# Causal attention in a decoder kernel: the next score before half an output tile instead of behind it

## The reference, cut to what matters

```
kqv = (x @ Wqkv + bqkv).reshape(b, s, 3, 16, 32)
q, k, v = kqv[:, :, 0], kqv[:, :, 1], kqv[:, :, 2]
scores = einsum('bsnh,btnh->bnst', k, q) / sqrt(32)
scores = triu(scores) + -10000.0 * tril(ones, k=-1)
attn = softmax(scores, axis=2)
out = einsum('bnkq,bknh->bqnh', attn, v).reshape(b, s, 512)
x = layernorm(x + out @ Wo + bo)
```

## Time and profile before

| what | value |
|---|---|
| median of 3 runs | 1642.73 us (1642.24 to 1643.59) |
| the profiled execution | 1642.21 us |
| its span, first to last instruction | 1640.4 us |
| mean granted TensorE clock | 0.985 |
| PE busy | 1543.4 us, 94% of the span |
| DVE busy | 1276.4 us, 78% |
| ACT busy | 950.1 us, 58% |
| POOL busy | 762.3 us, 46% |
| output halves of the causal stage (L2265), one matmul record | 593 ns median, 128 records |

### The profile page before, as it was taken

The page is one execution under the profiler, slowest core; times in us unless marked ns, Lnnn a source line. Parts: engine busy times, 40 slices in busy tenths (PEclk is TensorE's granted clock), DMA queues, the critical chain, the costliest instruction groups (busy, mean ns, idle before and its releaser), DMA issues. The chain is left out here.

```text
span 1640.4 us, 25463 instructions
## 1 busy us (share of the span) xinstructions
PE 1543.4 (94%) x8236; PEld 1102.4 (67%) x8268; DVE 1276.4 (78%) x2288; ACT 950.1 (58%) x1980; POOL 762.3 (46%) x729
## 2 busy tenths in 40 slices
PE   8999999999987999999889999999899999999996
PEld 5788886666634566666666767676467767777774
DVE  6467666767999999997678687887779999767573
ACT  3212325787877776677566665766535555555644
POOL 5043256778832554452633233232244266656564
PEclk9999999999998999999998999999999999999998
DMA  7200017543120000003422122222142100000000
GB/s 230 78 1 26 1 52 206 181 137 119 56 78 1 1 1 1 1 1 78 118 78 79 39 78 62 56 78 80 52 132 86 45 1 1 7 20 26 1 27 26
DMA packets 66999, 95.95 MB, mean 58 GB/s; under 512 B 11957, under 2 KB 28853, under 8 KB 66869
## 3 DMA queue, kind: packets, MB, share of 16 engines
q1 hardware_dynamic: 60196, 81.47, 16.2%
q0 software_dynamic: 6144, 12.60, 3.0%
q10 hardware_dynamic: 528, 0.26, 0.1%
HBM read 56.53 MB, written 4.19 MB: 37 GB/s over the span
## 5 line engine op out<-in xcount | busy, mean ns | idle before, releaser
L1931 ACT ACTIVATE causal_probs<-bank,causal_neg 128x512 f32<-128x512 f32 (+3 forms) x256 | 134.4, 530 | 127.9 <-DVE causal_neg L2026 102.8
L3206 PE MATMUL bank<-fp_xT,fp_weights_values 128*128 128x512 f32 x704 | 187.8, 403 | 7.3 <-DVE fp_gate L3100 5.0
L3206 PEld LDWEIGHTS bank<-fp_xT,fp_weights_values 128*128 128x128 f32 x704 | 128.4, 188 | 54.9 <-DVE fp_gate L3100 12.2
L1198 POOL DMA_DIRECT2D causal_qS<-causal_qk x96 | 48.6, 514 | 186.9 <-DVE causal_qk L1190 153.9
L3233 PE MATMUL bank<-fp_wd,fp_hT 128*128 128x512 f32 x528 | 133.8, 394 | 1.4 <-POOL fp_hT L2923 1.2
L3109 DVE SCALAR_TENSOR_TENSOR fp_up<-bank,fp_weights_scales,fp_up 128x512 f32<-128x512 f32 x132 | 99.1, 751 | 44.9 <-ACT fp_up L2992 37.4
L3233 PEld LDWEIGHTS bank<-fp_wd,fp_hT 128*128 128x128 f32 x528 | 98.6, 188 | 25.6 <-issue 3.4
L894 DVE TENSOR_REDUCE heads_neg<-bank 128x1 f32<-128x512 f32 x128 | 86.2, 676 | 37.7 <-PE bank L945 37.5
L1257 POOL TENSOR_TENSOR ternary_z<-ternary_z 128x1024 f32<-128x1024 f32 x16 | 38.8, 2425 | 151.6 <-DVE ternary_z L1470 142.8
L357 POOL TENSOR_TENSOR rope_qk<-rope_rot 128x512 f32<-128x512 f32 x32 | 43.0, 1343 | 142.5 <-DVE rope_rot L460 141.0
L1629 PE MATMUL bank<-weights_raw,ternary_qT 128*128 128x512 bf16 x432 | 104.3, 388 | 4.7 <-DVE ternary_z L1470 3.7
(11 more groups left out here) (289 smaller groups left out, 4265.4 us busy)
## 6 DMA issues: line engine op xcount, KB each, us to landing
pairs_xd<-X SPq DMA_DIRECT2D x64, 128.0 KB, 2.5
pairs_cd<-in_ctx SPq DMA_DIRECT2D x64, 128.0 KB, 2.7
causal_qS<-causal_qk SPq DMA_DIRECT2D x96, 64.0 KB, 2.8
causal_qS<-causal_qk POOLq DMA_DIRECT2D x96, 64.0 KB, 2.5
causal_kS<-causal_qk SPq DMA_DIRECT2D x96, 64.0 KB, 2.8
causal_kS<-causal_qk POOLq DMA_DIRECT2D x96, 64.0 KB, 2.7
X<-in_x SPq DMA_DIRECT2D x4, 1024.0 KB, 7.8
heads_cT<-in_ctxT SPq DMA_DIRECT2D x4, 1024.0 KB, 5.7
```

The source lines that it names most:

```text
L1931: act.activation(probs_of(i)[:, h + one], view[:, one], ACT.Exp, bias=neg[:, G % 2, at:at + 1], accum_out=total[:, G % 2, at:at + 1]).then ...
L3206: last = pe.matmul(banks[4 + g][:], values[:, g, n % NI, of], xT[:, part, g], start=part == 0, stop=part == 1)
```

## The change

In a step of PE's loop that has half an output tile, the next score is given first and the half behind it. In the other steps the order of instructions stays what it was. The waits inside `score` and `output` are the same, and no other engine's program is touched.

```diff
--- before.py
+++ after.py
@@ -2278,11 +2278,11 @@
             for n in range(GROUPS * STEPS + 9):
                 G, k = divmod(n, STEPS)
                 b, g = divmod(G, NF)
+                if n + 1 < GROUPS * STEPS:
+                    score(n + 1)
                 for past_b, t, half in out_at(n):
                     if half < 2:
                         output(past_b, t, OUT[t][1], half)
-                if n + 1 < GROUPS * STEPS:
-                    score(n + 1)
                 for u in range(NU - 1):
                     if (k - TURN[u]) % STEPS == 0 and 0 <= (n - TURN[u]) // STEPS < GROUPS:
                         turn((n - TURN[u]) // STEPS, u)
```

## The result

The kernel after took 1646.46 us (median of 10 runs, 1643.32 to 1647.66) against 1642.36 us of the kernel before on the same chip (10 runs, 1639.84 to 1644.71): ratio 1.0023, 95% interval 1.0015 to 1.0032. A second set gave 1644.95 us (12 runs) against 1642.59 (31 runs), ratio 1.0014 [1.0005, 1.0023]. So the change costs between 1 and 5 us, most likely 2 to 4, which is at the edge of what counts as a difference for this kernel.

A forecast was written before the change was run, and what follows sets the result against it. PE, busy 233.62 of 243.80 us, was taken as the bound. 1.4 + 1.8 - 1.3 = +1.9 us on the profiled 1642.21 gives 1644.1, with 0.5 to the runs' median: forecast 1644.6 us, range 1642.2 to 1648.4.

The forecast's parts named there:

- Tile 0: First halves of tile 0 (steps 65, 109, 153): score waits for exponentials, 0.46 us each, +1.4 us in all.
- Step 76: A first half of tile 1: score waits 1.67 us for a copy, projection's stall takes back 0.75, so +0.9 us.
- Step 120: A first half of tile 1: 0.46 us wait for exponentials, all inside the projection's 0.75 us stall, so 0.
- Step 164: A first half of tile 1, last group: score waits for its copy, no projection stall takes it back, +0.9 us.
- The other sixteen: Remaining moved steps, scores ready: score hides the half's first weight load, 0.08 x 16, so -1.3 us; other end 0.
- VectorE and ScalarE: They get 16 scores some 1.3 us sooner, but PE doesn't wait for them: worth nothing on the path.
- Rival 4: Earlier scores remove PE's waits for exponentials, 2.8 + 2.4 = 5.2 us, giving 1639.4 us; chance 0.05.
- Rival 5: Later stalls absorb the six delays, so nothing reaches the end, 1642.7 us; chance 0.12.
- Rival 1: Copies land late at steps 87, 120, 131, 164, first scores of a group: 3.7 us more, 1648.3; chance 0.12.
- Rival 2: Low-clock fall from 1159.2 us disappears (1642.6 us, chance 0.10) or a second one comes (1646.6, chance 0.08).
- Rival 3: In step 120 POOL's add takes the shared port first, delaying VectorE's minimum: about 0.5 us more, 1645.1; chance 0.05.

The follow-up runs named there:

- pool_later: Against before, same order: POOL's two adds of the output's bias wait for the group's third score instead of the first; 1639.38 us, ratio 0.9986.
- only_sixteen: Against before: first halves of tiles 0 and 1 stay ahead of the score, the other sixteen halves go behind it; 1642.65 us, ratio 0.9996.
- late_after: Against the kernel after: two small extra copies on SP's queue ahead of each group's six copies to kS; 1650.68 us, ratio 1.0055 (4 runs).
- only_six: Against before: only the six first halves of tiles 0 and 1 are given behind the score; 1647.54 us, ratio 1.0026.
- only_six_again: Second profile of the kernel with only the six first halves of tiles 0 and 1 moved, unchanged; one execution, 1643.68 us.
- again_before: The kernel before, unchanged, run and profiled a second time; 1642.1 us, ratio 0.9999.
- late_before: Against before, same order: two small extra copies on SP's queue ahead of each group's six copies to kS; 1643.27 us, ratio 1.0008.

## Why the prediction was right, and which step failed

The forecast was +1.9 us with no measurable change as the likeliest; the stretch showed +2.5, the medians +4.1 and +2.4. The first set lies just beyond the bound of 0.2% and the second within it; the range held both. What the medians have beyond 2.5 no profile explains; before alone spreads over 5 us in its runs, and which moments have the lower clock differs between executions. That part stays open.

- **Tile 0, 3 x 0.46 forecast: 0.52 each, 1.6 in all.** Right in mechanism and size. The score starts 0.15 us behind the end of the exponentials, 0.1 later than was allowed for.
- **Step 76, +0.9 forecast: +0.3.** The wait came as forecast: 1.96 us in after against the 0.37 for oT, and by the table step 76 is 2.08 - 0.52 = 1.56 later, forecast 1.67. The account of what takes it back failed here. I named one stall, 0.75 us, and 1.27 came back: 0.28 at step 78, where the score no longer starts right at the end of its exponentials and the transposes follow it sooner, 0.80 at step 79, the projection's stall, and 0.2 up to step 84. The projection at 960.97 has no wait any more.
- **Step 120, 0 forecast: +0.05.** Right. 0.53 late at step 120, 0.47 of it back by step 123.
- **Step 164, +0.9 forecast: +0.85.** Right: the score waits 1.27 us for its copy, and nothing takes it back.
- **The other sixteen, -1.3 forecast: 0. This is the step that failed.** I read 0.43 us from transposes to a half and 0.35 from transposes to a score and took the difference for a cost of that neighbourhood, which the move would avoid. Step 66 has 0.36 to the score now, as forecast, but then 0.32 from score to half and 1.72 from the half to the transposes: 2.40. Before it was 0.43, then 1.32 and 0.64 to the transposes: 2.39. A step without a half and without a wait has 0.35 + 0.32 (step 78 of pool_later) = 0.67 from transposes to transposes, so the half adds 1.72 = 4 x 0.43 us in either place, and the 0.43 ahead of it is no cost on top of that. The other end of the bound, zero, was the true one, and only_sixteen confirms it with 0.07 us over sixteen steps. The two misses, 1.3 too low here and 0.6 too high in step 76, partly cancelled, and that the sum came within 0.6 of the stretch is luck to that extent.
- **VectorE and ScalarE, nothing forecast: nothing.** Rival 4 (faster, 1639.4) falls with only_sixteen.
- **Rival 5 (nothing reaches the end) falls too:** 2.65 us are still there at step 168.
- **Rival 1, late copies:** in after the last copies of steps 87, 120 and 131 took 2.03, 2.03 and 2.02 us and were never in the way. late_after shows the mechanism real: +0.9 in steps 120 and 131, as priced.
- **Rival 2, the clock:** the fall of 1159.2 was neither gone nor doubled; in after it is at 0.64 in 1162.1 to 1167.2, and costs 0.37 us less. A further stretch at the lower level came elsewhere, in only_six behind a new wait of 1.81 us and in late_after behind one of 1.65, and not behind the waits of 1.80 in only_six_again, 1.86 in late_after and 1.96 in after. The page "TensorE: Matmul & The Clock Gate" of the Trainium skill, section "What's actually happening", which has the gate's windows run free of the kernel's start, agrees with a fall that is there in one execution of only_six and not in the next.
- **Rival 3, the port:** the tie in step 120 went VectorE's way, with the minimum at 1052.47, 0.16 us long, in after. The minimum that follows at 1054.24 was held up all the same, by POOL's second add: 0.84 us, where it had been 0.80 before. I had the mechanism and missed where it was already paid, in the minima of 0.80 us in before and at 1054.24, which pool_later prices at 0.5 us each in two batches. The page "SBUF — State Buffer" of the Trainium skill, section "SBUF: two separate sides", which says that the loser of the shared port waits out the other's instruction, agrees: 0.80 behind an add in before, 0.16 once the add was moved away.

## What to carry to other kernels

Where an engine works in order, ready work belongs in front of the instruction that may have to wait, not behind it: here, with half an output tile in front of the score, a copy 1.9 us later cost 0.2 and one 1.1 later nothing, and with the half behind the score two copies 1 us later cost 0.9 each. What a delay costs in the end is read from all the stalls downstream, short ones of 0.2 us included, and a stall that takes up a delay can itself be the trace of another fault, as 0.2 of the stall for x was of a port conflict four microseconds earlier. A gap between two instructions that differs by their neighbours is no saving until one knows to which of the two it belongs; the three intervals from one fixed point to the next have to be added up.

## What the runs showed of the hardware that was not expected

- A wait of 1.8 us of PE ahead of step 76's score was followed by a stretch at the lower clock in one execution of a kernel (granted clock 0.62, the half 3.19 us instead of 1.88) and by none in the next (1.00, 1.88). In late_after a wait of 1.65 us had such a stretch behind it (0.56) and a longer one, 1.86, had none (1.00).
- Half an output in float32 added 1.72 us to its step, both behind transposes and behind a score (2.39 and 2.40 us in all, 0.67 without a half), though the gap ahead of it was 0.43 in the one place and 0.32 in the other.
- The last copy to kS of step 76 landed 3.6 us after its issue in before (3.1 in again_before), and 2.4 us in late_before, where it was issued 1.0 us later behind two small extra ones: there the lateness at the issue was made good in the transfer.
- A VectorE minimum of 128x4 that met a GpSimd add took 0.80 us instead of 0.16, and cost PE 0.5 us downstream.
